# Two bias additions move from TensorE to GpSimd: output bias of the third cross attention, second bias of the first feed-forward

## The reference, cut to what matters

```
x = x + tanh(g_xattn[0]) * L0_xattn(layernorm(x), ctx, ...)   # ends in a feed-forward of its own
x = x + tanh(g_ffn[0])   * L0_ffn(layernorm(x))               # mixture of 8 experts
x = x + tanh(g_xattn[1]) * L1_xattn(...);  x = x + tanh(g_ffn[1]) * L1_ffn(...)
x = x + tanh(g_xattn[2]) * L2_xattn(layernorm(x), ctx, ...)   # ... return out @ Wo + bo
x = x + tanh(g_ffn[2])   * L2_ffn(...);    x = x + tanh(g_xattn[3]) * ...;  x = x + tanh(g_ffn[3]) * ...
```

```
h = gelu(layer_norm(X1) @ W1.T + b1);   y = layer_norm(X1 + h @ W2.T + b2) * g2 + be2
```

## Time and profile before

| | |
|---|---|
| median of 3 runs | 1419.97 us (1415.36 to 1420.51) |
| the profiled execution | 1427.67 us, its span 1425.7 us |
| busy of the span | PE 79%, PEld 54%, DVE 49%, ACT 43%, POOL 31% |
| mean granted TensorE clock | 0.866 of full |
| the L0f stage up to the last indirect DMA | 176 to 264 us |
| the L2 stage | 737 to 836 us |

### The profile page before, as it was taken

The page is one execution under the profiler, slowest core; times in us unless marked ns, Lnnn a source line. Parts: engine busy times, 40 slices in busy tenths (PEclk is TensorE's granted clock), DMA queues, the critical chain, the costliest instruction groups (busy, mean ns, idle before and its releaser), DMA issues. The chain is left out here.

```text
span 1425.7 us, 26533 instructions
## 1 busy us (share of the span) xinstructions
PE 1133.1 (79%) x8710; PEld 774.7 (54%) x8710; DVE 697.3 (49%) x3353; ACT 614.2 (43%) x1535; POOL 443.4 (31%) x636
## 2 busy tenths in 40 slices
PE   5998885499989999988987963997586999961684
PEld 3676744277745666653434742786452454441573
DVE  4564546133368776534553452111756788754002
ACT  3454453233369766423213230332462666630453
POOL 1674415333406455400002416343010000016343
PEclk8999987699999999999996865799685899975797
DMA  7499131222069920013530021454143222040343
GB/s 203 131 276 234 38 104 38 60 83 81 22 111 135 170 64 2 2 50 81 100 74 1 2 67 46 144 174 136 36 135 111 69 54 71 20 141 25 97 124 93
DMA packets 150262, 128.54 MB, mean 90 GB/s; under 512 B 13193, under 2 KB 126745, under 8 KB 150136
## 3 DMA queue, kind: packets, MB, share of 16 engines
q1 hardware_dynamic: 135256, 107.67, 31.4%
q0 software_dynamic: 7824, 15.47, 3.9%
q10 hardware_dynamic: 7056, 3.81, 1.0%
HBM read 88.91 MB, written 40.85 MB: 91 GB/s over the span
## 5 line engine op out<-in xcount | busy, mean ns | idle before, releaser
L304 POOL TENSOR_TENSOR L_Z<-L_Z,L_mx 128x512 f32<-128x512 f32 x84 | 88.5, 1055 | 271.1 <-DVE L_mx L615 271.1
L3070 DVE CUSTOM_DVE_ANT_0 L3s_masked<-L3s_psS,L3s_trilw 128x512 f32<-128x512 f32 (+3 forms) x256 | 109.1, 487 | 35.0 <-PE L3s_psS L2969 34.5
L863 ACT ACTIVATE L_Z<-L_Z,L_nmx 128x154 f32<-128x154 f32 x256 | 105.1, 414 | 42.0 <-DVE L_nmx L913 41.9
L3041 ACT ACTIVATE L3s_E<-L3s_psT 128x512 f32<-128x512 f32 (+1 forms) x192 | 87.9, 531 | 49.8 <-PE L3s_psT L2982 49.5
L732 POOL TENSOR_TENSOR L_Z<-L_Z,L_rin 128x488 f32<-128x488 f32 x64 | 64.0, 1000 | 111.8 <-DVE L_rin L921 111.8
L615 DVE CUSTOM_DVE_ANT_0 L_Z<-L_psS,L_Z 128x154 f32<-128x154 f32 x256 | 63.4, 313 | 57.6 <-PE L_psS L352 45.9
L774 PE MATMUL L_psS<-L1k_G,L_xnT 128*128 128x462 f32 x192 | 82.4, 525 | 2.8 <-DVE L_nmx L913 1.4
L913 DVE CUSTOM_DVE_ANT_0 L_Z<-L_psS,L_mask 128x154 f32<-128x154 f32 x256 | 67.7, 313 | 11.2 <-PE L_psS L774 10.7
L513 ACT ACTIVATE L_E<-L_psT 128x512 f32<-128x512 f32 x84 | 46.1, 596 | 57.2 <-PE L_psT L365 57.2
L2969 PE MATMUL L3s_psS<-L3s_KS,L3s_QS 72*128 72x512 bf16 (+3 forms) x256 | 55.9, 336 | 11.4 <-PEq L2955 8.5
L931 DVE COPY L_PT<-L_psT 122x512 f32<-122x512 f32 x64 | 43.6, 682 | 40.4 <-PE L_psT L784 39.5
(11 more groups left out here) (543 smaller groups left out, 2857.5 us busy)
## 6 DMA issues: line engine op xcount, KB each, us to landing
L_Z<-in_fside_Bx16xSxS SPq DMA_DIRECT2D x16, 1232.0 KB
L2f_w<-in_L_ffn_W SPq DMA_DIRECT2D x39, 256.0 KB
slotsL<-empty SPq DMA_DIRECT2D x1, 8320.5 KB, 68.4
L1m_cb<-comb_rows SPq DMA_DIRECT2D x8, 1024.0 KB
L3f_w<-in_L_ffn_fc_w SPq DMA_DIRECT2D x32, 256.0 KB
L0f_w<-in_L_ffn_W SPq DMA_DIRECT2D x24, 256.0 KB
q_parts<-L3s_parts SPq DMA_DIRECT2D x12, 384.0 KB, 5.3
L3s_QS<-q_parts SPq DMA_DIRECT2D x16, 288.0 KB
```

What stands on the lines that cost most here:

```text
L304: nc.gpsimd.tensor_tensor(Z[:, t % NZ, h, 0:KM_], Z[:, t % NZ, h, 0:KM_], top.broadcast_to([P, HG, KM_]), ALU.subtract).then_inc(z_ready, 1)
L863: last = nc.scalar.activation(Z[:, t % 2, h], Z[:, t % 2, h], ACT.Exp, scale=-1.0, bias=nmx[:, t % 2, h:h + 1], accum_out=sums[:, t % 2, h ...
L3041: nc.scalar.activation(E[:, g.par, h, EO[group[0]]:EO[group[0]] + wd], psT[:, k, 0:wd], ACT.Exp).then_inc(t_free, 1)
L3070: last = nc.vector.tensor_tensor_reduce(masked[:, k, at:at + wd], psS[:, k, at:at + wd], trilw[:, S - wd:S], 1.0, LOW, ALU.add, ALU.max, m ...
```

## The change

Both bias matmuls go, and GpSimd adds the biases ahead to what DVE later adds the product to: b2 to X1, gate times bo (`gbo`) to X. In the L2 stage GpSimd makes its additions after all eight normalisations have read X, and before its first subtraction; DVE's residuals wait for them on `xb_ready`. In L0f its four new additions stand ahead of the four old ones, each after the normalisation of its group, and DVE's `output(k)` waits on `b2_ready`. No DMA is added or moved.

```
+            gbo = sb("gbo", [P, D])
...
+            if late:
+                nc.gpsimd.tensor_scalar(gbo[:], m.wide("L2_xattn_bo"), m.gate(c["gate"]), None, ALU.mult).then_inc(gbo_ready, 1)
+                pool.wait_ge(gbo_ready, 1)
+                pool.wait_ge(xn_ready, LN)
+                for b in range(B):
+                    x = m.X[:, b * TB:(b + 1) * TB]
+                    nc.gpsimd.tensor_tensor(x, x, gbo[:].unsqueeze(1).broadcast_to([P, TB, D]), ALU.add).then_inc(xb_ready, 1)
             for t in range(NTL):
...
-                        last = pe.matmul(o, x, wo, start=(i == 0), stop=(not late and i == len(parts) - 1), skip_group_check=True)
-                        if late:
-                            last = pe.matmul(o, m.ones[0:1, :], m.row("L2_xattn_bo"), start=False, stop=(i == len(parts) - 1),
-                                             skip_group_check=True)
+                        last = pe.matmul(o, x, wo, start=(i == 0), stop=(i == len(parts) - 1), skip_group_check=True)
...
+                    dve.wait_ge(xb_ready, tiles[t][0] + 1)
...
+                    dve.wait_ge(xb_ready, B)
...
+        b2 = m.wide("L0_xattn_b2").unsqueeze(1).broadcast_to([P, TB, D])
+        for k in range(TB):
+            pool.wait_ge(self.x1_ready, k + 1)
+            x = m.X1[:, k * TB:(k + 1) * TB]
+            nc.gpsimd.tensor_tensor(x, x, b2, ALU.add).then_inc(self.b2_ready, 1)
         pool.wait_ge(self.gg_ready, 2)
-        pool.wait_ge(self.x1_ready, TB)
...
-                pe.matmul(self.psY[:, k % 2].rearrange("p (t d) -> p t d", d=D), m.ones[0:1, :],
-                          m.row("L0_xattn_b2").unsqueeze(1).broadcast_to([1, TB, D]), start=True, stop=False, skip_group_check=True)
...
-                    last = pe.matmul(o, self.h[:, k % 2, j, i * P:(i + 1) * P], self.w2[:, j], start=False,
+                    last = pe.matmul(o, self.h[:, k % 2, j, i * P:(i + 1) * P], self.w2[:, j], start=(i == 0 and j == 0),
...
+            dve.wait_ge(self.b2_ready, k + 1)
```

More of the change, by code:

```diff
@@ L257, in quad_attention @@
         v_clear, vr_full = sem("v_clear"), sem("vr_full")
+        gbo_ready, xb_ready = (sem("gbo_ready"), sem("xb_ready")) if late else (None, None)
         block = ctx.enter_context(nc.Block())
@@ L1515, in __init__ @@
             sem(s) for s in ("gg_ready", "xb_ready", "var2_ready", "std2_ready"))
+        self.b2_ready = sem("b2_ready")
     def sync(self, sp):
```

## The result

The changed kernel takes 1406.8 us (median of 6 runs, 1402.76 to 1409.83) against 1418.42 (6 runs, 1415.36 to 1420.51) for the kernel before on the same chip. The ratio is 0.9913 with a 95% interval of 0.9896 to 0.9931: 12.3 us faster (9.8 to 14.8), where 8.8 was forecast. The profiled execution took 1408.04 us, span 1406.1.

What follows compares the result with a forecast made beforehand. L0f was taken as bound by when DVE delivers `slot_to` to POOL's scatters, L2 by PE's written order. Gains of 2.3 (L0f) and 6.5 us (L2), together 8.8, from the median 1419.97 gave 1411.2 us; range 1405 to 1418.5.

Steps and rivals of the forecast that it cites:

- 4 x 0.42 = 1.7, all on the path: L2, collected tile's first projection: four bias matmuls removed at the upper clock save 1.7 us, since DVE waits.
- 4 x 0.73 = 2.9: L2, collected tile's second projection: four bias matmuls removed at the lower clock save 2.9 us, while nobody else works.
- The tail after it, priced 2.0: L2, last four tiles: one bias matmul fewer each, three at 0.42 and one at 0.73 us, saves 2.0 us.
- Rival 5: Bias matmul's price isn't its slot; following products take over part, L2 gives 4 instead of 6.5 us: 1413.7; chance 0.10.
- Rival 1: L2's low-clock stretch does more or less: gain 7.6, 10.0 or 12 us; chance 0.60 shared with forecast and Rival 3.
- I take 2.3; bounds 1.05 and 3.0.: L0f: removing four 512-column bias matmuls brings `slot_to` of groups 1 and 2, and so POOL's end, 2.3 us sooner.
- rival 2: L0f: PE's pauses lower the clock for 10 us, 4.3 lost; net gain 4.5, 1415.5 us; chance 0.15.
- Rival 3: L0f: stall ahead of `slot_to` ends with POOL's sending; groups 1 and 2 gain 1.8, total 8.3 us; shares 0.60.
- Rival 4: L0f: that stall grows to 8.3 us ahead of groups 1 and 2; 5.9 us slower, 1425.9; some size, chance 0.08.
- Costs taken as nothing: L0f and L2: POOL's additions, DVE's longer normalisations and new waits stay hidden; waits at most 0.1 us each, 0.9.
- "before 187" and "before 192": L0f, expected profile: POOL's new 1.26 us additions end before 187 us, its old four before 192.
- a change of over 2 us in such a stage as a sign of error: Any stage without an edit: a change of more than 2 us would show the prediction wrong.

Runs made afterwards that it cites:

- e5: Kernel before, order of matmuls kept, but L2's bias comes from identity times broadcast bias over 128 rows instead of one; 1423.88 against 1433.8 us, ratio 0.9947.
- e6: Changed kernel with four 128x512 copies on DVE ahead of the residual of the collected tile's first projection in L2; ratio 0.9936 to the kernel before.
- e7: Changed kernel with the four new bias additions in L0f started only after all of DVE's normalisations; ratio 0.9891 to the kernel before.

## Why the prediction was right, and where it was off

**Sign and size.** Faster, 12.3 us instead of 8.8; 1406.8 lies in the range of 1405 to 1418.5. The place was right: alone, the two edits gave 10.2 and 4.4 us. The mechanism was right in kind, but its larger part, L2, was priced at little more than half of what it was worth, and the clock was what made up most of the rest.

**L2, "y" and "y2".** The term "4 x 0.42 = 1.7, all on the path" was too small: 4.90 us between the two projections became 2.65, 2.25 less. The term "4 x 0.73 = 2.9" was far too small: from the second projection to the next transpositions (line 391, now 400) 8.53 us became 2.53, 6.0 less. The tail after it, priced 2.0, gave 3.05. Together 11.3 for 6.6. Two things were missing. First, a slot was taken as the price of one matmul, but a bias matmul also made the product behind it pay for the change of rows. Rival 5 had this interplay with the sign reversed, "the products behind it would take over part of it"; its counter-argument, that the steps with and without ones are equal, was the very sign of it: both kinds paid. e5 prices it, 0.42 against 0.22. The Trainium skill, TensorEngine Tiling (Array Packing), "Key Properties", states a rule that may bear on it: changing the tiling mode drains the engine. The trace agrees if a 1-row and a 128-row matmul count as different modes, with 0.20 us for each change; the page gives no figure, and no run here shows that they do count so.

Second, the clock. Rival 1 had the case that happened, "if the low stretch never comes, some 3 us more: 12"; it was given as a variant and not as the centre. e5, with every bias matmul present, keeps the clock up and gets 8.9 of the 11.3 us. Between before and e5 the first projection, at the upper clock in both, shrinks by 1.34 us (4.90 to 3.56, seven changes of 0.19), and a tile of the tail by 0.19: 1.34 + 1.34 + 4 x 0.19 = 3.4 us for the changes of rows; the other 5.5 are put down to the clock by subtraction, not measured by themselves. e6 shows the clock's fall without a bias matmul in the projections, at 1.6 us.

**L0f.** "I take 2.3; bounds 1.05 and 3.0." POOL's first indirect DMA came 1.8 us sooner (mean of seven profiles with the edit, 38.3, against 40.1 of five without), as counted. For the last one it depends on the stall: 3.3 sooner without it (78.9 against 82.2), a little above the upper bound, and 1.8 with it (83.3 against 85.1). Rival 3 is thus what happened in five of the seven profiled kernels with this edit: its condition, that the stall's end is tied to POOL's sending and not to DVE's arrival, agrees with the times (the end stays at 11.4 to 11.7 us after the first DMA while DVE arrives at 8.4 instead of 9.8), the stall grows by some 1.3 us, and groups 1 and 2 move by 1.8. The 6.5 us between the two profiles is an unedited one with the stall beside an edited one without it.

**Rivals 2 and 4.** The clock in L0f after the change is 0.98 over 193.3 to 235.0, the stretch that answers to the earlier trace rows shifted by 5.3 us: no low stretch of 10 us. (It falls at 233.7, when POOL is sending already; before it fell at 232.1.) The stall grew from 1.8 to 3.1 us, not by 6.4. Of the stalls that followed in L2f the first was 6.9 and 8.3 us without L0f's edit and 6.2 to 8.3 with it, the second 9.6 in both kernels without and 9.6 to 11.7 with it; two kernels are too few to say whether that is the edit's. Rival 4 has its mechanism in L0f and not its size. In L2 taking matmuls out did the opposite of what rival 2 feared: the clock stayed at 1.00 where it had fallen.

**Costs taken as nothing.** The wait list added no idle of DVE at lines 641, 648, 652 or 1657 that names POOL. POOL's additions cost DVE 2.8 us in L0f and 3.5 in L2 (four copies of 0.86 to 1.12 us instead of 0.17), all under cover, as e7 shows for L0f. The forecast said additions ended "before 187" and "before 192"; they ended at 193.4 and 198.3, which is 5.3 for the later start of the stage and 1 us more.

**A stage without an edit.** The prediction named a change of over 2 us in such a stage as a sign of error. It happened three times, +5.3 ahead of L0f and -3.1 and -4.3 behind L2, so this sign says little here. The +5.3 lies within the spread of that stretch over the profiles. So does the -3.1: from L2's last residual to L3f it is 419.1 to 424.2 us in the profiles with the stall and 414.9 to 420.5 in those without, which overlap. The -4.3 goes with the stall that the profile of before had and that of after had not: L3f takes 167 to 171 us in every profile with the stall and 162 to 164 in every one without, whatever was edited. Why L3f is longer there wasn't tried.

## What to carry to other kernels

A one-row matmul between full ones costs more than its own slot: it also makes its neighbour pay, here 0.2 us each way. Two cures need no other engine: grouping (3.8 us of the stage here, of which the whole kernel didn't show enough to tell) and spreading the row over 128 partitions (8.9 us of the stage, 7.6 of the kernel). Moving the addition to an idle engine gave the most, 11.3 us of the stage. On a path where TensorE and VectorE take turns, a delay of 2 us can also lower the granted clock and cost nearly as much again; price both. Before you read a difference stage by stage, check that the two profiles agree in the stages that weren't touched.

## What the runs showed of the hardware

- fp32 matmuls of 128x128 at the upper clock: steps of 0.22 us in e5's row of eight; 0.25 to 0.27 each in groups of four, the step to the next group included, whether over 128 rows or over one; 0.42 each where 1 row and 128 rows alternate; one of 1x512 takes as long as four of 1x128 (1.12 and 1.15 us).
- The second projection at the granted clock 0.54: 2.04 us for what takes 1.16 at 1.00.
- The granted clock fell from 1.00 to 0.50 among sixteen alternating 1-row and 128-row matmuls without a wait of PE, in ten profiles of ten; it stayed at 1.00 over the same sixteen in groups of four, in two of two.
- The stall called "remote", in all six profiles of two chips and in none of the four of a third, ended 11.4 to 11.7 us after POOL's first indirect DMA in seven profiles. So it was longer (3.0 to 3.2 us instead of 1.7 and 1.9) where DVE came to it sooner after that DMA.
